# Embedding stage: the shift of text steps 5 to 10 on GpSimd, and the rest of W1 taken behind the last step

## The reference

```python
emb = W_word[input_ids] + W_pos[position_ids] + W_type[...] + ...      # nine tables
mu = mean(emb); var = mean((emb - mu)**2)
text = (emb - mu) * rsqrt(var + EPS) * ln_gamma + ln_beta              # 64 x 77 rows of 192
...
h = gelu(einsum('nsr,nskrh->nskh', z, W1[sidx, topi]) + b1g)           # later, in the third stage
```

## Time and profile before

| | us |
|---|---|
| median of 3 runs | 1391.14 (1389.05 to 1392.76) |
| the profiled execution | 1391.86 |
| its span in the trace | 1390.1 |

### The profile page before, as it was taken

One profiled execution on the slowest core, in us unless ns is written; L12 is line 12 of the kernel. 1 busy time (PEld: TensorE's weight loads), 2 busy tenths in 40 slices (PEclk: granted clock), 3 DMA queues, 4 the chain that ended last, 5 costly groups with the idle time before them and its releaser, 6 DMA issues.

```text
span 1390.1 us, 34218 instructions
## 1 busy us (share of the span) xinstructions
PE 1228.7 (88%) x12232; PEld 625.1 (45%) x12232; DVE 1104.9 (79%) x3371; ACT 1086.3 (78%) x2696; POOL 995.5 (72%) x712
## 2 busy tenths in 40 slices
PE   2953799999999999858999999999999999999996
PEld 2941466666666666522343333333343333333332
DVE  5592488888888888957888888888888888888884
ACT  0244467777677767539999999999999999999994
POOL 7641367756776676617888888888888888788884
PEclk7975899999999999969999999999999999999998
DMA  9564313222222222134214222232413323232410
GB/s 268 152 136 81 59 34 100 63 69 74 95 72 67 73 92 69 51 86 108 64 44 89 65 70 64 57 70 54 101 41 87 69 59 64 56 77 53 95 38 12
DMA packets 95705, 107.06 MB, mean 77 GB/s; under 512 B 12772, under 2 KB 92668, under 8 KB 95254
## 3 DMA queue, kind: packets, MB, share of 16 engines
q1 hardware_dynamic: 86576, 94.95, 26.3%
q10 hardware_dynamic: 6848, 6.13, 2.6%
q0 software_dynamic: 2112, 3.79, 1.1%
HBM read 67.88 MB, written 33.71 MB: 73 GB/s over the span
## 4 chain that ended last, share of the span: by engine, by line
PE 21%; ACT 18%; DVE 12%; issue 3%; POOL 0%; POOLq 0%; DVEq 0%
DVE arena L1474 11%; ACT ring L1073 11%; PE ring L1736 9%; PE code L1749 9%; ACT arena L1085 6%; PE ring L1768 2%; PE ring L1759 1%; DVE arena L1482 0%; ACT arena L1081 0%; POOL arena L817 0%; POOLq L157 0%; PE ring L1586 0%; PE ring L1634 0%; DVE arena L1257 0%; DVEq L1473 0%
## 5 line engine op out<-in xcount | busy, mean ns | idle before, releaser
L1474 DVE TENSOR_TENSOR arena<-ring,arena 128x496 f32<-128x496 f32 x1008 | 611.4, 668 | 123.4 <-ACT ring L1073 123.4
L817 POOL TENSOR_TENSOR arena<-arena 128x992 f32<-128x992 f32 x264 | 611.7, 2330 | 121.1 <-ACT arena L1085 111.6
L1073 ACT ACTIVATE ring<-ring 128x496 f32<-128x496 f32 x1008 | 544.9, 688 | 16.9 <-PE ring L1736 16.0
L1736 PE MATMUL ring<-arena,w_stack 99*32 99x496 bf16 x6144 | 423.9, 375 | 23.5 <-DVE arena L1474 17.7
L1749 PE MATMUL code<-arena,w_pad 128*32 128x496 f32 x3072 | 389.6, 581 | 8.3 <-DVE arena L1482 8.0
L1736 PEld LDWEIGHTS ring<-arena,w_stack 99*32 99x32 bf16 x6144 | 163.5, 95 | 399.6 <-DVE arena L1474 220.3
L1085 ACT ACTIVATE arena<-ring 128x992 f32<-128x992 f32 x252 | 283.9, 1127 | 0.7 <-PE ring L1736 0.7
L1578 PE MATMUL ring<-arena 96*128 96x372 f32 x384 | 135.3, 490 | 1.5 <-ACT arena L929 0.9
L1749 PEld LDWEIGHTS code<-arena,w_pad 128*32 128x32 f32 x3072 | 97.5, 110 | 59.6 <-DVE arena L1474 22.5
L753 POOL TENSOR_TENSOR arena<-arena 128x372 f32<-128x372 f32 x96 | 91.9, 986 | 32.7 <-DVE arena L1314 32.7
L1578 PEld LDWEIGHTS ring<-arena 96*128 96x128 f32 x384 | 71.7, 194 | 62.3 <-ACT arena L937 15.9
(11 more groups left out here) (143 smaller groups left out, 1437.1 us busy)
## 6 DMA issues: line engine op xcount, KB each, us to landing
arena<-gates SPq DMA_DIRECT2D x48, 496.0 KB, 6.7
gates<-arena SPq DMA_DIRECT2D x16, 744.0 KB, 11.5
arena<-h_scratch SPq DMA_DIRECT2D x32, 279.0 KB
arena<-z_parts SPq DMA_DIRECT2D x144, 62.0 KB, 2.7
h_scratch<-arena SPq DMA_DIRECT2D x16, 279.0 KB
z_parts<-arena SPq DMA_DIRECT2D x48, 93.0 KB, 2.1
arena<-h_scratch SPq DMA_DIRECT2D x12, 372.0 KB
out_h<-arena SPq DMA_DIRECT2D x12, 372.0 KB
```

Of the source, the lines that this page charges most:

```text
L817: p_.tensor_tensor(spaces[quad % SPACES][:, j:j + 2], hid[:, POOL_DUOS.index(duo) % 2], gst[:, block // EB, j:j + 2], ALU.mult).then_inc(s ...
L1073: a_.activation(product, product, ACT.Gelu_apprx_tanh).then_inc(s_hid, 1)
L1474: v_.tensor_tensor(spaces[quad % SPACES][:, j + p], duo_bank(duo, p), gst[:, block // EB, j + p], ALU.mult).then_inc(s_gat, 1)
L1736: mm = t_.matmul(bank[32 * q:32 * q + 32], w1s[:, x + 32 * q:x + 32 * q + 32], zst[:, o, j + p], start=True, stop=True)
```

## The change

- A constant `BETA_ON_POOL = 5`. For steps 0 to 4 nothing changes.
- For steps 5 to 10 `scaled` writes into `tout` in SBUF, where it wrote back into PSUM. It now waits for the earlier store of that buffer, which `shifted` waited for before. `shifted` is gone from DVE for these steps.
- POOL adds beta in place in `tout` (`beta_added`, one instruction of 112 x 768). It stands ahead of `text_rstd` of the next step: the shift of step j-1, then the 1/sqrt of step j, then the gathers of step j+4 while there are any. That of step 10 stands last.
- SP's stores of steps 5 to 10 wait for POOL's add. `mean_off` of steps 6 to 10 waits for `scaled` of the step before, where it waited for `shifted`.
- DVE takes the rest of W1 behind `scaled` of step 10. ACT's cast of part 1 moves behind its last copies of W2, and DVE's part 2 follows as before.

```diff
+BETA_ON_POOL = 5
             def store_text(jj, par):
-                wait_apart(sp, (s_to, jj + 1))
+                if jj < BETA_ON_POOL:
+                    wait_apart(sp, (s_to, jj + 1))
+                else:
+                    wait_apart(sp, (s_tb, jj - BETA_ON_POOL + 1))
...
+            def beta_added(jj):
+                pool.wait_ge(s_tmul, jj + 1)
+                pool.wait_ge(s_gb, 16 * 2)
+                x = tout[:, jj % 2]
+                p_.tensor_tensor(x, x, tbet.unsqueeze(1).to_broadcast([TT, 4, D]), ALU.add).then_inc(s_tb, 1)
...
             for jj in range(2, JJ):
+                if jj > BETA_ON_POOL:
+                    beta_added(jj - 1)
                 text_rstd(jj)
                 if jj + 4 < JJ:
                     gather(jj + 4)
+            beta_added(JJ - 1)
...
                 act.wait_ge(s_tneg, jj + 1)
-                wait(act, s_to, jj)
+                if jj <= BETA_ON_POOL:
+                    wait(act, s_to, jj)
+                else:
+                    wait(act, s_tmul, jj)
...
-                if jj == 9:
-                    act.wait_ge(s_ws, 1)
-                    a_.copy(w1h[:, 1], w1r)
-                    a_.copy(b1h[:, 1], b1r).then_inc(s_wc, 1)
-
+            act.wait_ge(s_ws, 1)
+            a_.copy(w1h[:, 1], w1r)
+            a_.copy(b1h[:, 1], b1r).then_inc(s_wc, 1)
             stage1_over(act)
...
                 dve.wait_ge(s_xm, jj + 1)
                 dve.wait_ge(s_trs, jj + 1)
+                if jj >= BETA_ON_POOL:
+                    wait(dve, s_todma[par], use_count(jj, par))
                 for bb in range(4):
                     x = normed()[:, bb // 2, D * (bb % 2):D * (bb % 2) + D]
-                    last = v_.scalar_tensor_tensor(out=x, in0=x, scalar=trs[:, bb:bb + 1],
+                    out = tout[:, par, bb] if jj >= BETA_ON_POOL else x
+                    last = v_.scalar_tensor_tensor(out=out, in0=x, scalar=trs[:, bb:bb + 1],
                                                    in1=tgam, op0=ALU.mult, op1=ALU.mult)
...
-                if old:
+                if old and jj <= BETA_ON_POOL:
                     shifted(jj - 1, 1 - par)
...
+            text_step(9, 1)
+            text_step(10, 0)
+            scaled(10, 0)
             dve.wait_ge(s_wc, 1)
...
             last.then_inc(s_ws, 1)
-            text_step(9, 1)
-            text_step(10, 0)
-            scaled(10, 0)
-            shifted(10, 0)
             dve.wait_ge(s_wc, 2)
```

More of the change, by code:

```diff
@@ L367, in build @@
         s_tmv, s_tve, s_trs, s_tn = sem("text_moments"), sem("text_var_eps"), sem("text_rstd"), sem("text_normed")
-        s_tmul, s_to = sem("text_scaled"), sem("text_ready")
+        s_tmul, s_to, s_tb = sem("text_scaled"), sem("text_ready"), sem("text_biased")
         s_todma = [sem("text_stored0"), sem("text_stored1")]
```

## The result

The changed kernel took 1395.03 us in the median of 18 runs (1391.95 to 1399.01), the kernel before 1390.7 us in 18 runs beside it. The ratio is 1.0033, with a 95% interval of 1.0022 to 1.0044: slower by 4.3 us, where +3.3 was forecast.

The account below looks back on a forecast made before the run. Stage 1 bounds: POOL in steps 6 and 7, then the chain through DVE with W1's rest. -2.6 for step 10's `scaled`, +4.1 store's wait, +1.8 tail give +3.3: 1394.4 us, range 1389.5 to 1399.3 (the forecast's own 1392 to 1396).

Parts of the forecast that it names:

- POOL term: POOL's adds ahead of the 1/sqrt, 1.87 us each: `scaled` of step 7 at 89.1, of step 8 at 94.2.
- Rival D: POOL's adds in steps 5 to 10 nearer 1.4 than 1.9 us; 1388 without the store's wait, chance 0.06.
- unobstructed S(10): Start of `scaled` of step 10 without the store's wait: 103.8, 2.6 us earlier than 106.38.
- store's wait: `scaled` of step 10 waits for step 8's store behind two 512 KB parts: 107.9 instead of 103.8, +4.1 us.
- tail: From `scaled` of step 10 to stage 2's first statistics: 14.9 us instead of 13.1, +1.8; bounds 13.0 to 14.9.
- A: Rival: step 8's store gets through in time, `scaled` of step 10 starts at 103.8; 1390.3 us, chance 0.17.
- B: Rival: queues alternate, step 8's store also waits for the third part; `scaled` of step 10 at 112.0, 1398.5 us, chance 0.25.
- Rival C: POOL's last add, starved by DVE's five subtractions, ends 3.9 us later; 1397.9 us with the store's wait; chance 0.09.
- Stages 2 and 3 were moved and not changed: Behind stage 1: the remaining 1270 us from stage 2's first statistics move as one block, their times unchanged.

## Why the prediction was right

In the order of its steps, all from E:

- **The POOL term held.** An add took 1.81 to 1.84 us, 1.87 taken. S(7) moved by +3.6 (+3.8 forecast), S(8) by -1.9 (-1.6), S(9) by -2.3 (99.0 less 101.07, -2.1). Rival D falls with it.
- **The unobstructed S(10) held.** Without the parts it is 32.5, 2.6 us earlier than 35.1, and -2.6 was the term.
- **The store's wait was the right mechanism and 1.0 us too small.** S(10) is 5.1 us behind its unobstructed place, not 4.1. The term had the second part done 9.5 us after the first was issued (96.1 to 105.6). In the kernel before, a part that runs alone lands 6.6 us after its issue; in the changed kernel the second of the two took 10.5 us from its issue at 96.09, and so landed 11.3 us after the first was issued. The store behind them needed less than the 2.3 us taken for it, 1.1. The one came 1.8 us later than forecast and the other took 1.2 less; that they partly cancel is luck. The rest, 0.4 us, is the first part's issue, 25.2 from E instead of 24.8. The prediction also had the store issued behind both parts; its first transfer went out 0.1 us ahead of the second, which changes nothing, as the last of the four decides. A (S(10) at 32.5 from E) and B (at 40.7) both fall. B's condition did arise: the third part was issued at 100.85, while the second was still on its way until 106.6. Yet the store of step 8 was in by 107.63, and the third part landed 10.9 us after its issue, at 111.7. The prediction also tied B, which is about whole transfers taking turns, to a rule about packets taking turns; the two are not the same, and packets in turn could have let a small store through beside a part.
- **The tail was 14.6, not 14.9.** POOL's add and DVE's subtractions do keep each other out, and one add cost DVE 1.5 us rather than its whole 1.87. The bounds 13.0 and 14.9 were the two ends that the runs show, 13.1 without the add and 14.6 with it.
- **Rival C did not happen in this kernel and does in the one with the adds alone.** The add of step 10 took 2.52 us and got in behind one instruction. In its neighbour it took 4.38, behind two. What I had against C, a power that got in behind one instruction, was thin.
- **Stages 2 and 3 were moved and not changed**, within what one execution varies.

The sum of the measured terms is -2.6 + 5.1 + 1.5 = +4.0, against -2.6 + 4.1 + 1.8 = +3.3. The chance of 0.43 for slower by over 0.3%, and 0.53 for within it, was fair to a result of 1.0033 whose interval has the bound inside.

Where I was most wrong, it was in an experiment: I expected the adds alone to move stage 2 by 1.7 us, and it was 5.75. I had left S(10) nearly where it was, and so forgot my own POOL term for steps 6 and 7, of which 2.5 us arrive at S(10) there; and I had taken the last add at its length alone, where it was held back by 2.6 us. The change of reader, from `shifted` to `scaled`, made the wait for the store 0.6 us even with one part ahead of it.

## What to carry to other kernels

Work out a store's slack from both of its ends before you move work between engines: an extra stage between the result and the store, and an earlier first write into its buffer, both eat it. Large transfers that were harmless when engine work kept them apart stand in front of a small urgent one once that work is gone, so list every issue on every queue at the new times, and take for a transfer its time from issue to landing and not bytes by rate. Work moved from a busy engine is worth most in a gap where the receiving engine is idle anyway: here W1's rest fitted there, and the shifts of steps 5 and 6 did not.

## What the runs showed of the hardware

- Transfers that ACT and SP issued on their own queues landed nearly in the order of their issue across both, so that a 512-KB transfer held up the store transfers issued just behind it. In the kernel with only the rest moved they landed at 102.2 (issued 93.6), 103.8 (512 KB, issued 94.1) and 104.7 (issued 97.5). The order is not strict. In the kernel without POOL's last add, the transfers that SP issued at 101.5 and ACT (512 KB) at 101.0 have these rows:

```profile
L556 SPq DMA_DIRECT2D h_scratch<-arena x1: 597/597/597, 101.5 to 101.5; - x1
...
DMA to landing us min/median/max: 9.9/9.9/9.9
L885 ACTq DMA_DIRECT2D w_stack<-arena x1: 554/554/554, 101.0 to 101.0; - x1
...
DMA to landing us min/median/max: 10.8/10.8/10.8
```

  So the later and smaller one landed 0.4 us ahead. The Trainium skill, page "DMA: Bandwidth & Descriptors", section "Queues, rings and completion order", says that a DMA engine takes turns between the queues, packet by packet; these landings do not show it.
- A POOL add with both operands in SBUF, beside DVE instructions with two SBUF inputs, took 1.81 us alone, 2.52 when it got in behind one of them (which cost DVE 1.5), and 4.38 when it got in only behind a second one of 2.27 us. The Trainium skill, page "SBUF — State Buffer", section "Who interferes with whom", says that two such instructions exclude each other, and these times agree. Whether POOL got in between two DVE instructions was not the same in the two cases, and the runs don't say why.
